# Both halves of a tile's scores issued one behind the other, the transposes of P behind them

## The chip, the cores and the metric

One core of a Trainium2 chip runs the whole program. The metric is the device time of one execution in microseconds (us); three executions of the kernel before gave a median of 1829.21 us.

## The reference

A network of two layers over `x` of shape (4, 512, 128). Each layer adds `s * silu(g)` to `x`, where `s` is a mixer and `g` a network, both computed from the layer-normed `x`. The change lies in the network of the first layer: six blocks of windowed attention (16 heads of 64, windows of 32 tokens, each query sees its own and the previous window) and a gated feed-forward part.

```python
def attn_layer(x, Wqkv, qs, ksc, Wo):
    q, k, v = heads(x @ Wqkv)                 # 16 heads of 64
    q, k = l2norm(q) * qs, l2norm(k) * ksc    # then rotary turn with a scale
    sim = einsum('bhwie,bhwje->bhwij', bq, look(bk)) * 8.0     # windows of 32, look: previous + own
    attn = softmax(where(mask, -max, sim), -1)
    out = einsum('bhwij,bhwje->bhwie', attn, look(bv))
    return out.reshape(b, n, INNER) @ Wo
for i in range(6):
    x = attn_layer(shift_tokens(x), ...) + x
    x = ffn_layer(shift_tokens(x), ...) + x
```

## The kernel before

`build_network` writes out, by hand, one instruction order for each engine. The unit of work is a tile of 128 tokens (four tiles to a batch, four batches, six blocks: 96 tiles). The engines all walk through the same numbered stages `g`; in stage `g` TensorE projects q, k and v of tile `g`, transposes q and k of tile `g-1` and forms its scores, transposes the softmax P of tile `g-2`, and multiplies P with v of tile `g-3` (`attend`). A round is the four tiles of one batch in one block. The work of a round that is no longer per tile is spread over the stages behind it, by the remainder of `g` by 4:

- remainder 2: the output projection in two halves, `output_projection(out_0, 0)` (called wo0 below) and `output_projection(out_1, 1)` (wo1), 16 matmuls each;
- remainder 3: `ffn_centre` and `ffn_variance`, the two matmuls of the layer norm; here `transpose_p(g-2, 0)` stands ahead of both score halves, and the halves already follow one another;
- remainder 0: `ffn_up` in three parts, in between the rest;
- remainder 1: `ffn_down`.

The names used below. **S0 and S1** are `scores(g-1, 0)` and `scores(g-1, 1)`, line 589: 64 small matmuls each, with a weight load to each, contraction over 64 rows, 32 columns of the array. They write `sc_ps`. Only S1's last matmul signals (`sc_full`), and S0 carries all the waits. **T0 and T1** are `transpose_p(g-2, 0)` and `transpose_p(g-2, 1)`, line 603: four 128x128 transposes each, each half waiting for its half of P (`p_scaled`, GpSimd line 496) and for a bank of `ring`.

`ring` is two PSUM banks taken in turn by everything in `stage_fills`; a fill waits until the fill two before it has been copied out. In stages of remainder 3 the fills end xc, p0, var, p1, so T1 waits for the copy of T0's output (`copy_pT(g-2, 0)`, ScalarE line 784). In stages of remainder 1 T1 waits for `add_ffn` (VectorE line 996).

VectorE's order in a stage: `add_attention(out_1, 1)` (line 973, only in remainder 3, it waits for wo1), then `row_max(g-2)` (lines 916, 918, 927; it waits for `sc_full`), `rotate` of k (951, 955), `sum_squares` of k (965), `row_sum(g-2)` (934, 939), `rotate` and `sum_squares` of q. ScalarE's end of a stage is `inverse_norms(g)` (lines 799, 801, 805; it waits for both sums of squares) and only behind it `copy_pT(g-2, 0)` (784), `inverse_deviation`, `copy_pT(g-2, 1)`. GpSimd scales P (496) after `row_sum`.

Of the kernel before, what the change touches and what calls it, by code (L numbers as in the profile page):

```python
# [267 lines left out]
def build_network(nc, block, signals, tail, weights, after, norm, state):  # L268
# [3 lines left out]
    with ctx:  # L272
# [81 lines left out]
        def tile_there(g):  # L354
            return 0 <= g < TILE_COUNT

        def round_at(g, s, later):

            r = g // TILES - later
            return r if g % TILES == s and 0 <= r < ROUNDS else None  # L360
# [161 lines left out]
        def _(pe):  # L522
# [14 lines left out]
            def project_q(g, f):  # L537

                if f == 1:
                    if g % (B * TILES) == 0:  # L540
                        pe.wait_ge(s_wq, 16 * (g // (B * TILES) + 1))
                    state_there(g)
                    if g > 0:
                        pe.wait_ge(q_sq, g)
                        pe.wait_ge(q_rot, 2 * g)
                nc.tensor.matmul(qk_ps[:, f, :], tile_of(g), quarter(wqkv, f), start=True, stop=True).then_inc(q_full, 1)  # L546

            def project_k(g, f):
                if f == 1:
                    if g % (B * TILES) == 0:  # L550
                        pe.wait_ge(s_wk, 16 * (g // (B * TILES) + 1))
                    state_there(g)
                    if g > 0:
                        pe.wait_ge(k_sq, g)
                        pe.wait_ge(k_rot, 2 * g)
                nc.tensor.matmul(qk_ps[:, 2 + f, :], tile_of(g), quarter(wqkv, 2 + f), start=True, stop=True).then_inc(k_full, 1)  # L556

            def project_v(g, f):
                if f == 0:
                    if g % (B * TILES) == 0:  # L560
                        pe.wait_ge(s_wv, 16 * (g // (B * TILES) + 1))
                    state_there(g)
                nc.tensor.matmul(ring_bank("v", g, f), tile_of(g), quarter(wqkv, 4 + f), start=True, stop=True).then_inc(v_full, 1)  # L563

            def transpose_qk(g, f):

                pe.wait_ge(qk_scaled, 4 * g + scale_at[f] + 1)
                to = ring_bank("t", g, f)
                for n in range(4):
                    c = 4 * f + n  # L570
                    ins = nc.tensor.transpose(to[:, n * P:(n + 1) * P], qkn[:, c * P:(c + 1) * P], ident[:, :])  # L571
                ins.then_inc(qkT_full, 1)

            def scores(g, f):

                t = g % TILES
                if f == 0:
                    if g == 0:
                        pe.wait_ge(c_dve, 8)
                        pe.wait_ge(tail.s_there.sem, 2 * TILES)  # L580
                    pe.wait_ge(qkT_copied, 4 * (g + 1))
                    if g == 1:
                        pe.wait_ge(sc_sub, 2)
                    if g > 1:
                        pe.wait_ge(oT_copied, 2 * (g - 1))
                for pair in range(4 * f, 4 * (f + 1)):
                    for q in range(TW):
                        for par in range(2):
                            ins = nc.tensor.matmul(  # L589
                                sc_ps[WIN * q:WIN * (q + 1), par, 64 * pair:64 * (pair + 1)],  # L590
                                qT[64 * par:64 * (par + 1), pair, WIN * q:WIN * (q + 1)],
                                kT[64 * par:64 * (par + 1), pair, P * t + WIN * q:P * t + WIN * (q + 2)],
                                start=True, stop=True)
                if f == 1:
                    ins.then_inc(sc_full, 1)
# [49 lines left out]
            def ffn_up(r, c):  # L645
                m = FCH[c]
                if c == 0:
                    pe.wait_ge(s_wffn, 48 * (r // B + 1))
                    pe.wait_ge(xn_ready, r + 1)
                nc.tensor.matmul(ring_bank("gate", r, c)[0:m, :], w1[:, FF + P * c:FF + P * c + m], xn[:, :],  # L650
                                 start=True, stop=True).then_inc(gate_full, 1)
                nc.tensor.matmul(ring_bank("lin", r, c)[0:m, :], w1[:, P * c:P * c + m], xn[:, :],
                                 start=True, stop=True).then_inc(lin_full, 1)
# [8 lines left out]
            for g in range(STAGES):  # L662
                out_0 = round_at(g, 2, 1)
                out_1 = round_at(g, 2, 1)
                centre = round_at(g, 3, 1)
                spread = round_at(g, 3, 1)
                up = round_at(g, 0, 2)
                down = round_at(g, 1, 2)
                if g == 0:
                    tail.turn_out(pe, 1)  # L670
                if tile_there(g):
                    project_k(g, 1)
                    project_k(g, 0)
                    if g == 1:
                        tail.turn_out(pe, 2)
                    project_v(g, 0)
                if g == 0:
                    pe.wait_ge(tail.r_og.sem, TILES)
                if g == 1:
                    tail.out_product(pe, 2)  # L680
                if tile_there(g - 1):
                    transpose_qk(g - 1, 3)
                if tile_there(g):
                    project_q(g, 1)
                if tile_there(g - 1):
                    transpose_qk(g - 1, 2)
                if g == 1:
                    tail.turn_out(pe, 3)
                if tile_there(g):
                    project_q(g, 0)  # L690
                if g == 1:
                    tail.out_product(pe, 3)
                if up is not None:
                    ffn_up(up, 0)
                if tile_there(g - 3):
                    attend(g - 3, 0)
                if tile_there(g - 1):
                    transpose_qk(g - 1, 1)
                if g == 0:
                    tail.out_product(pe, 1)  # L700
                if tile_there(g):
                    project_v(g, 1)
                if up is not None:
                    ffn_up(up, 1)
                if tile_there(g - 3):
                    attend(g - 3, 1)
                if tile_there(g - 1):
                    transpose_qk(g - 1, 0)
                if down is not None:
                    ffn_down(down)  # L710
                if centre is not None:
                    ffn_centre(centre)
                if g == TILE_COUNT + 3:

                    pe.wait_ge(q_sq, TILE_COUNT)
                    pe.wait_ge(k_sq, TILE_COUNT)
                    pe.wait_ge(q_rot, 2 * TILE_COUNT)
                    pe.wait_ge(k_rot, 2 * TILE_COUNT)
                    norm.centre(pe, 0, qk_ps[:, 0, :], centre_w)
                    norm.centre(pe, 1, qk_ps[:, 1, :], centre_w)  # L720
                if up is not None:
                    ffn_up(up, 2)
                if out_0 is not None:
                    output_projection(out_0, 0)
                if tile_there(g - 2) and centre is not None:
                    transpose_p(g - 2, 0)
                if tile_there(g - 1):
                    scores(g - 1, 0)
                if tile_there(g - 2) and centre is None:
                    transpose_p(g - 2, 0)  # L730
                if out_1 is not None:
                    output_projection(out_1, 1)
                if tile_there(g - 1):
                    scores(g - 1, 1)
                if spread is not None:
                    ffn_variance(spread)
                if g == TILE_COUNT + 3:
                    norm.centre(pe, 2, qk_ps[:, 2, :], centre_w)
                    norm.variance(pe, 0, qk_ps[:, 3, :], mean_w)
                if g == TILE_COUNT + 4:  # L740

                    pe.wait_ge(oT_copied, 2 * TILE_COUNT)
                    norm.variance(pe, 1, sc_ps[:, 0, :], mean_w)
                    norm.variance(pe, 2, sc_ps[:, 1, :], mean_w)
                if tile_there(g - 2):
                    transpose_p(g - 2, 1)
# [1675 lines left out]
```

## Time and profile before

| | |
|---|---|
| median of three executions | 1829.21 us (1826.84 to 1832.83) |
| span of the profiled execution | 1822.0 us |
| time outside the span, by the median | 7.2 us |
| TensorE matmul busy | 96% |
| VectorE busy | 80% |
| GpSimd busy | 65% |
| ScalarE busy | 64% |
| mean granted TensorE clock | 0.986 |

The span is counted from the first to the last instruction of one profiled execution; the executions that gave the median were timed as a whole, so the 7.2 us hold what lies around the span and the scatter of single executions. A busy TensorE is not TensorE at its peak: the share counts a matmul from its start to its modelled end.

### The profile page before, as it was taken

The page shows a single profiled execution, that of the slowest core. Times are in us where ns is not written, and L with a number is a line of the kernel's source. Part 1 is how long each engine was busy: PE and PEld are TensorE (multiplying, and loading weights), DVE is VectorE, ACT ScalarE, POOL GpSimd, SP SyncE. Part 2 cuts the span into 40 slices and gives each one's busy share as a digit, 9 for nine tenths or more (in the row PEclk, how much of TensorE's full clock was granted, in tenths as well). Part 3 has the DMA queues.
Part 4 walks back from the last instruction along what each step waited for, and adds up shares of the span by engine and source line. Part 5 has one row for each costly group of instructions (what it writes and reads, how often), then busy time and mean ns, then how long its engine had stood idle before and what let it go on. Part 6 is the DMA issues. An engine that isn't in the chain of part 4 may idle for free. (4 is left out here: it accounts for less than half of the span.)

```text
span 1822.0 us, 70687 instructions
## 1 busy us (share of the span) xinstructions
PE 1755.0 (96%) x30348; PEld 1136.7 (62%) x30348; DVE 1454.4 (80%) x1677; ACT 1162.8 (64%) x2032; POOL 1190.7 (65%) x1285
## 2 busy tenths in 40 slices
PE   7988999999999999999999999999999999998788
PEld 6855665665666566566666666656656656665466
DVE  6488789888788888888868978888887887896485
ACT  4356667667666765766766766676576676675644
POOL 1059678787677777767767867777776777775000
PEclk9899999999999999999999999999999999999999
DMA  4023222323222333223223223223223232222031
GB/s 151 1 50 77 58 72 66 92 66 80 73 68 68 95 78 73 73 57 98 73 67 80 68 64 98 67 69 80 72 60 91 70 81 69 65 68 74 1 71 47
DMA packets 87669, 128.94 MB, mean 71 GB/s; under 512 B 26776, under 2 KB 32800, under 8 KB 87360
## 3 DMA queue, kind: packets, MB, share of 16 engines
q1 hardware_dynamic: 87360, 124.43, 26.6%
q8 instruction: 242, 3.96, 1.0%
q14 instruction: 67, 0.55, 0.1%
HBM read 25.70 MB, written 1.11 MB: 15 GB/s over the span
## 5 line engine op out<-in xcount | busy, mean ns | idle before, releaser
L488 POOL TENSOR_TENSOR lent<-t,lent 128x1024 f32<-128x1024 f32 x192 | 455.2, 2371 | 356.7 <-DVE lent L955 356.6
L479 POOL TENSOR_TENSOR lent<-lent,rn 128x512 f32<-128x512 f32 x384 | 400.7, 1075 | 13.8
L619 PEld LDWEIGHTS sc_ps<-shared,v_win 64*64 64x64 f32 x12288 | 198.0, 135 | 147.1 <-issue 146.1
L791 ACT ACTIVATE sq<-qk_ps 128x1024 f32<-128x1024 f32 x192 | 196.1, 1021 | 94.9 <-PE qk_ps L556 94.2
L571 PEld LDWEIGHTS ring<-ident,lent 128*128 128x128 f32 x1536 | 176.5, 141 | 118.5 <-issue 76.8
L571 PE MATMUL ring<-ident,lent 128*128 128x128 f32 x1536 | 241.7, 280 | 5.7 <-POOL lent L479 5.3
L496 POOL TENSOR_TENSOR shared<-shared,rden 128x512 f32<-128x512 f32 x192 | 196.4, 1044 | 68.8 <-DVE rden L939 68.8
L784 ACT COPY shared<-ring 128x512 f32<-128x512 f32 x192 | 111.3, 580 | 198.2 <-PE ring L603 197.5
L955 DVE TENSOR_TENSOR lent<-qk_ps,rot 128x1024 f32<-128x1024 f32 x192 | 232.5, 1211 | 0.0
L965 DVE TENSOR_REDUCE sums<-sq 128x16 f32<-128x1024 f32 x192 | 231.7, 1207 | 0.0
L951 DVE TENSOR_TENSOR t<-qk_ps,rot 128x1024 f32<-128x1024 f32 x192 | 229.2, 1194 | 1.9 <-ACT sq L791 1.8
L619 PE MATMUL sc_ps<-shared,v_win 64*64 64x32 f32 x12288 | 219.1, 221 | 4.1 <-DVE shared L927 3.4
L546 PE MATMUL qk_ps<-wqkv,state 128*128 128x512 f32 x384 | 197.8, 597 | 0.2 <-DVE shared L1538 0.2
L563 PE MATMUL ring<-wqkv,state 128*128 128x512 f32 x384 | 196.9, 594 | 0.0
L589 PEld LDWEIGHTS sc_ps<-kT,qT 64*32 64x32 f32 x12288 | 136.9, 105 | 82.9 <-issue 77.0
L589 PE MATMUL sc_ps<-kT,qT 64*32 64x64 f32 x12288 | 166.2, 224 | 17.2 <-issue 11.8
L556 PE MATMUL qk_ps<-wqkv,state 128*128 128x512 f32 x384 | 182.2, 597 | 0.5 <-issue 0.5
L916 DVE TENSOR_TENSOR sc_ps<-sc_ps,mask_f 128x1024 f32<-128x1024 f32 x96 | 118.3, 1232 | 77.8 <-PE sc_ps L589 76.9
L634 PE MATMUL ring<-shared,wo 128*128 128x256 f32 x768 | 173.6, 379 | 0.0
L754 ACT COPY shared<-sc_ps 128x512 f32<-128x512 f32 x192 | 113.0, 589 | 71.3 <-PE sc_ps L619 71.3
L634 PEld LDWEIGHTS ring<-shared,wo 128*128 128x128 f32 x768 | 142.2, 190 | 17.4
L973 DVE TENSOR_TENSOR xa<-ring,state 64x256 f32<-64x256 f32 x96 | 40.6, 423 | 131.8 <-PE ring L634 130.3
(213 smaller groups left out, 2736.4 us busy)
## 6 DMA issues: line engine op xcount, KB each, us to landing
v_win<-v_tok SPq DMA_DIRECT2D x1488, 64.0 KB, 2.0
wqkv<-in_w_qkv SPq DMA_DIRECT2D x18, 512.0 KB, 3.7
spread<-gate_rows SPq DMA_DIRECT2D x32, 128.0 KB, 3.7
wo<-in_w_o SPq DMA_DIRECT2D x6, 512.0 KB, 3.8
w<-in_w SPq DMA_DIRECT2D x6, 341.0 KB, 3.3
w<-in_w SPq DMA_DIRECT2D x6, 192.0 KB, 3.0
r_xtok<-in_x SPq DMA_DIRECT2D x4, 256.0 KB, 3.9
out_x<-xo SPq DMA_DIRECT2D x4, 256.0 KB, 2.3
```

The lines of the kernel that those rows point to most:

```text
L479: nc.gpsimd.tensor_tensor(by_head(quarter(qkn, f)), by_head(quarter(qkn, f)), rn[:, 8 * f:8 * (f + 1)].unsqueeze(2).to_broadcast([P, 8, DH ...
L488: nc.gpsimd.tensor_tensor(half(qkn, k), half(t1, k), half(t2, k), ALU.add).then_inc((q_added, k_added)[k], 1)
L496: nc.gpsimd.tensor_tensor(by_head(quarter(pn, f)), by_head(quarter(pe_, f)), rden[:, 8 * f:8 * (f + 1)].unsqueeze(2).to_broadcast([P, 8, D ...
L546: nc.tensor.matmul(qk_ps[:, f, :], tile_of(g), quarter(wqkv, f), start=True, stop=True).then_inc(q_full, 1)
L563: nc.tensor.matmul(ring_bank("v", g, f), tile_of(g), quarter(wqkv, 4 + f), start=True, stop=True).then_inc(v_full, 1)
L571: ins = nc.tensor.transpose(to[:, n * P:(n + 1) * P], qkn[:, c * P:(c + 1) * P], ident[:, :])
L589: ins = nc.tensor.matmul(sc_ps[WIN * q:WIN * (q + 1), par, 64 * pair:64 * (pair + 1)], qT[64 * par:64 * (par + 1), pair, WIN * q:WIN * (q ...
L619: ins = nc.tensor.matmul(sc_ps[64 * par:64 * (par + 1), part, P * pair + WIN * q:P * pair + WIN * (q + 1)], v_win[64 * part:64 * (part + 1 ...
L634: ins = nc.tensor.matmul(to[:, 0:2 * P], wo[:, c, :], oT[:, c, 2 * P * f:2 * P * (f + 1)], start=(c == 0), stop=(c == PAIRS - 1))
L951: nc.vector.tensor_tensor(by_head(half(t1, k)), by_head(of), rot[:, l % 2, 2 * k, s:s + 1, :].to_broadcast([P, HEADS, DH]), ALU.mult).then ...
L955: nc.vector.tensor_tensor(half(t2, k).rearrange("p (h s d) -> p h s d", s=2, d=DH // 2), swapped, rot[:, l % 2, 2 * k + 1, s:s + 1, :].to_ ...
L965: nc.vector.tensor_reduce(sums[:, HEADS * k:HEADS * (k + 1)], by_head(half(sq, k)), AX.X, ALU.add).then_inc(sums_ready, 1)
```

## The change

In each stage S1 moves to directly behind S0. In the stages of remainder 0 and 1 the order S0 T0 S1 T1 becomes S0 S1 T0 T1. In the stages of remainder 2 wo0 S0 T0 wo1 S1 T1 becomes wo0 S0 S1 T0 wo1 T1. In the stages of remainder 3 (T0 S0 S1 var T1) nothing changes. The order of the ring's fills, all waits and the orders of the other engines stay.

```diff
                 if tile_there(g - 1):
                     scores(g - 1, 0)
+                if tile_there(g - 1):
+                    scores(g - 1, 1)
                 if tile_there(g - 2) and centre is None:
                     transpose_p(g - 2, 0)
                 if out_1 is not None:
                     output_projection(out_1, 1)
-                if tile_there(g - 1):
-                    scores(g - 1, 1)
                 if spread is not None:
                     ffn_variance(spread)
```

## Rows read from the trace of the kernel before

**Rows 1.** The page: the span, and each engine's busy time and instruction count.
```profile
span 1822.0 us, 70687 instructions
PE 1755.0 (96%) x30348; PEld 1136.7 (62%) x30348; DVE 1454.4 (80%) x1677; ACT 1162.8 (64%) x2032; POOL 1190.7 (65%) x1285
```

**Rows 2.** Timeline (start us, us, engine, line), end of a stage of remainder 1.
```profile
968.10 0.86 PE L589 MATMUL sc_ps<-kT,qT 64*32 64x64 f32 x64
968.20 1.53 DVE L996 SCALAR_TENSOR_TENSOR state<-ring,col,xa 64x512 f32<-64x512 f32 x2 [0.56 <-PE ring L659]
...
969.47 0.86 PE L589 MATMUL sc_ps<-kT,qT 64*32 64x64 f32 x64
...
970.75 1.88 PE L556 MATMUL qk_ps<-wqkv,state 128*128 128x512 f32 x4
```

**Rows 3.** Timeline, TensorE, end of a stage of remainder 2.
```profile
983.64 0.87 PE L589 MATMUL sc_ps<-kT,qT 64*32 64x64 f32 x64
984.43 0.66 PE L603 MATMUL ring<-ident,shared 128*128 128x128 f32 x4
984.93 3.62 PE L634 MATMUL ring<-shared,wo 128*128 128x256 f32 x16
988.48 0.86 PE L589 MATMUL sc_ps<-kT,qT 64*32 64x64 f32 x64
989.27 0.66 PE L603 MATMUL ring<-ident,shared 128*128 128x128 f32 x4
989.76 1.88 PE L556 MATMUL qk_ps<-wqkv,state 128*128 128x512 f32 x4
```

**Rows 4.** Timeline, TensorE, end of the stage behind it (remainder 3).
```profile
1000.03 0.63 PE L603 MATMUL ring<-ident,shared 128*128 128x128 f32 x4
...
1000.58 1.56 PE L589 MATMUL sc_ps<-kT,qT 64*32 64x64 f32 x128
...
1002.08 1.12 PE L643 MATMUL ring<-xsq,mean_w 128*128 128x512 f32 x2
...
1003.06 0.63 PE L603 MATMUL ring<-ident,shared 128*128 128x128 f32 x4
```

**Rows 5.** Timeline, VectorE, GpSimd and ScalarE from wo1 to that last transpose.
```profile
988.58 0.88 DVE L973 TENSOR_TENSOR xa<-ring,state 64x256 f32<-64x256 f32 x2 [3.96 <-PE ring L634]
...
989.52 1.23 DVE L916 TENSOR_TENSOR sc_ps<-sc_ps,mask_f 128x1024 f32<-128x1024 f32 x1
...
998.22 2.05 POOL L496 TENSOR_TENSOR shared<-shared,rden 128x512 f32<-128x512 f32 x2 [0.17 <-DVE rden L939]
...
1000.26 1.21 DVE L965 TENSOR_REDUCE sums<-sq 128x16 f32<-128x1024 f32 x1
...
1001.50 0.33 ACT L799 ACTIVATE raised<-sums,low_col 128x32 f32<-128x32 f32 x1
...
1002.35 0.57 ACT L784 COPY shared<-ring 128x512 f32<-128x512 f32 x1
```

**Rows 6.** The page: instruction fetch (DMA queues) and the scores' matmuls (costliest groups).
```profile
q8 instruction: 242, 3.96, 1.0%
L589 PE MATMUL sc_ps<-kT,qT 64*32 64x64 f32 x12288 | 166.2, 224 | 17.2 <-issue 11.8
```

**Rows 7.** Timeline, TensorE, holes inside a burst of scores: two of remainder 3, one of 0.
```profile
931.44 1.44 PE L589 MATMUL sc_ps<-kT,qT 64*32 64x64 f32 x114
935.25 0.34 PE L589 MATMUL sc_ps<-kT,qT 64*32 64x64 f32 x14 [2.37 <-issue]
...
1395.91 0.45 PE L589 MATMUL sc_ps<-kT,qT 64*32 64x64 f32 x29 [1.37 <-issue]
...
1547.97 0.38 PE L589 MATMUL sc_ps<-kT,qT 64*32 64x64 f32 x18 [1.51 <-issue]
```

**Rows 8.** Timeline and stretches (busy us by engine, PEclk, DMA): clock behind the first hole.
```profile
937.20 3.29 PE L556 MATMUL qk_ps<-wqkv,state 128*128 128x512 f32 x4
936.50:940.00 3.50, 3.50 (x9) 1.95 (x8) 3.43 (x5) 1.79 (x3) 2.72 (x3) 0.52 0.38 97
```

## The prediction

> **What bounds the kernel now.** First the page: TensorE is busy for 96% of the span, the next engine, VectorE, for 80% [rows 1]. So nearly all of the time is TensorE's own queue, and a step taken out of it counts in full where no other engine's result arrives just as late. Then the timeline of each kind of stage, to price a step from start to start, since the modelled ends overlap. Then, for each wait that TensorE passes near the change, how long the awaited work had been done. Last the holes in which TensorE waits for no engine ("issue").
>
> Two things stand beside TensorE's own work. **A chain that is exactly as late.** In a stage of remainder 3, T1 starts 0.14 us after the end of copy_pT(0) (1002.35 + 0.57 = 1002.92, T1 at 1003.06) [rows 4, 5]. That copy stands on ScalarE behind inverse_norms, which starts at 1001.50, 0.03 us after VectorE's last sum of squares (1000.26 + 1.21 = 1001.47). VectorE has run without a gap since it took up wo1's sums at 988.58. So wo1 is the head of a chain: wo1, VectorE's whole stage, inverse_norms, the copy, T1. From wo1's start (984.93) to T1 (1003.06) it takes 18.13 us [rows 3, 4]. I read the same distance in all 23 such rounds: from copy to T1 it is 0.14 to 0.30 us in 17 of them, 0.41 in one, and 1.6 to 4.0 in the five in which a hole kept TensorE back first. 0.14 is the smallest, and where it stands TensorE comes up to 0.03 us later behind var than its own pace would have it, so 0.14 is the latency and TensorE and the chain tie.
>
> **Holes of instruction supply.** Scores run at 11 ns a matmul, each with a load. Inside such bursts TensorE stops for up to 2.6 us with nothing to wait for [rows 6, 7]. The fetch queue moved 3.96 MB in 242 packets, 16.4 KB each, for 60,696 loads and matmuls [rows 1, 6], one packet for 251 of them, and with the waits in between one for 256. Numbering the queue's records by start, all 12 holes within bursts fall on the same point of the 256. So they are late blocks. Where they stop, the block's packet had landed 1.2 to 1.5 us before; it starts typically 0.8 us after the block before it began to be used and takes 0.9 to 1.5 us. A block thus needs some 3 to 4 us, and 256 instructions used up faster than that make a hole.
>
> **The change part by part.** (1) Fewer changes between scores and transposes on TensorE. Before, the tail of a stage is S0 and T0 1.37, S1 and T1 1.28 = 2.65 us (968.10 to 970.75) [rows 2]. Both score halves together, up to the next operation, take 1.50 (1000.58 to 1002.08) [rows 4], where two apart take 2 x 0.79 [rows 3]. A transpose half ahead of ordinary work takes 0.49, ahead of scores 0.55 to 0.59 [rows 2 to 4]. After: 1.50 + 0.49 + 0.49 = 2.48, a gain of 0.17. In the stages of remainder 2, wo1 takes 3.55 ahead of scores; at its step of 0.216 (3.62 less a last 0.38, over 15) it takes 3.46 ahead of T1: 0.79 + 0.50 + 3.55 + 0.79 + 0.49 = 6.12 becomes 1.50 + 0.50 + 3.46 + 0.49 = 5.95, again 0.17 [rows 3]. 72 stages change (24 of remainder 0, 23 of 1, 24 of 2, and the one of 3 that has no centre): **-12.2 us**. T0 directly before T1 isn't in the trace. At 0.44, its shortest case, it would be -16; at 0.59, as ahead of scores, -5.
>
> (2) wo1 is moved. With S1 ahead of it, it starts and ends 1.50 - 0.79 = 0.71 later in 23 rounds. VectorE starts add_attention on it, as before (3.96 us idle ahead of it [rows 5]), so T1 of the next stage can't start before +0.71, while TensorE, 0.17 early, arrives at -0.17. Per round TensorE waits 0.88 less the slack above. 18 rounds have 0.00 to 0.27 of it, 0.7 us together: 18 x 0.88 - 0.7 = **+15.1 us**; in the five with a hole the wait lies within the hole. Bounds: 0 if VectorE could start its stage early, 23 x 0.88 = 20 if no hole covers. I take 15, since all 23 chains measure alike. Behind T1 nothing of it is given back: k's projections, T1's successors, stand in the same queue.
>
> (3) More and longer holes. The stretch S0 T0 S1 took 0.79 + 0.59 + 0.79 = 2.16 us; now 128 scores take 1.50, and in the remainder-2 stages wo1 no longer parts them. I laid the 242 blocks over the new order and kept each block's supply time as traced: holes grow from 17 to 24 us. With supply times drawn at random from those traced, the growth is 5 to 12. I take **+6.5 us**, with 0 and +20 as bounds: the high end comes from the stages of remainder 3, where scores already run as 128: five of 23 have a hole of 1.4 to 2.6 us within the burst [rows 7], far more than the others.
>
> (4) Clock. Behind the 2.37 us hole TensorE runs at a granted 0.52, its lower level, and k's four matmuls take 3.29 in place of 1.88 us [rows 2, 8]; behind the holes of up to 2.0 us it does not fall. One more fall, some 1.5 us, is possible; taken at nothing.
>
> (5) At nothing: T0 0.7 later (its copy isn't late for attend, a stage away, nor for v's bank, over 1.5 us behind T1); T1 0.17 earlier (in remainder 1 it waits for add_ffn, done at 969.73, its own start 970.26 [rows 2, 3]: 0.53 of cover, and without it at most 0.17 x 23 = 4); T0 of remainder 3, whose half of P is done at 999.24, 0.79 ahead of it [rows 4, 5]: 0.88 later that is 0.1 to 0.15 late, but it lies within the wait at T1. row_max starts up to 0.7 earlier in the stages of remainder 1 and 2, which only gives VectorE slack. No DMA is issued by what moves, and SP, GpSimd, VectorE and ScalarE keep their order. The one wait that grows is T1's of remainder 3. Behind it stand T1 and the next stage's projections; for those wait squares and rotate.
>
> **Sum**, against the span of 1822.0: -12.2 + 15.1 + 6.5 = +9.4, so 1831.4. With 7.2 around it by the median, 1829.2 + 9.4 = **1838.6 us**.
>
> [...] Holes of over 1.3 us stand in the middle of bursts [rows 7]. [...]
>
> **Rivals.** (A) TensorE alone decides: the chain gives way, because VectorE makes up the 0.71, and holes grow little. -12.2 + 3 = -9, 1820. For it: 96% busy, VectorE only 80%. Against it: VectorE is gapless for 12 us in just this stage. 0.07. [...] (B) The chain binds, but holes don't grow, or T0 to T1 runs at 0.44: 1829.2 - 12.2 + 15.1 = 1832, down to 1829 with the shorter step, within 0.3%. 0.17. (C) Slower by holes above all: the changed stages come near the rate of those of remainder 3, +20 for term (3) and some falls of the clock. It decides once a block of 256 takes longer than 1.5 us plus what is queued before it, as those rows show it can: 1829.2 + 2.9 + 20 + 3 = 1855. 0.06. (D) The forecast, slower by 6 to 18 us: 0.70. That the change doesn't do what it says is hardly possible here, since TensorE keeps the order of its matmuls.
>
> **How the numbers follow.** 0.3% is 5.5 us, about what a measurement of this kernel can tell from no change. Faster: A, 0.07. Same: B, 0.17, and little of D. Slower: D and C, 0.76. The forecast's own range, from its terms' bounds, is 1833 to 1847. Leaving out A's lower half and C, the range is 1829 to 1848.
>
> **What would show it.** In the profile after: from S to the next operation 1.50 in changed stages, T0 to T1 0.49; wo1 starting 1.50 + 0.50 behind S0; 18.13 from wo1 to T1 unchanged; TensorE waiting about 0.7 to 0.9 us ahead of T1 in remainder 3, on the copy of line 784; rounds longer by about a third of a microsecond where no hole falls; holes of line 589 adding up to 20 to 30 us, some now in stages of remainder 2. It would be wrong if VectorE's stage behind wo1 became shorter than 12 us, if T0 and T1 waited for each other, or if holes came where none is computed.

## The result

The changed kernel takes 1837.38 us (median of 22 executions) against 1830.71 us for the kernel before (22 executions): 0.42% slower, with a 95% interval of 0.27% to 0.57%, that is 5 to 10 us. Forecast were 9.4 us more and 1838.6 us. The change loses by one mechanism and gains by another, as laid out in the prediction; the sizes are compared below. Two single executions of the kernels tried below (3534 and 3411 us, near twice the others) are left out of every ratio.

The page of the changed kernel, first lines and three of its costliest groups:

```profile
span 1835.8 us, 70687 instructions
PE 1754.4 (96%) x30348; PEld 1144.5 (62%) x30348; DVE 1454.9 (79%) x1677; ACT 1161.6 (63%) x2032; POOL 1190.6 (65%) x1285
...
L589 PE MATMUL sc_ps<-kT,qT 64*32 64x64 f32 x12288 | 162.4, 225 | 25.6 <-issue 20.4
...
L973 DVE TENSOR_TENSOR xa<-ring,state 64x256 f32<-64x256 f32 x96 | 40.6, 423 | 158.2 <-PE ring L634 156.7
...
L916 DVE TENSOR_TENSOR sc_ps<-sc_ps,mask_f 128x1024 f32<-128x1024 f32 x96 | 118.3, 1232 | 42.7 <-PE sc_ps L589 41.4
```

The same two groups of VectorE on the page of the kernel before:

```profile
L916 DVE TENSOR_TENSOR sc_ps<-sc_ps,mask_f 128x1024 f32<-128x1024 f32 x96 | 118.3, 1232 | 77.8 <-PE sc_ps L589 76.9
L973 DVE TENSOR_TENSOR xa<-ring,state 64x256 f32<-64x256 f32 x96 | 40.6, 423 | 131.8 <-PE ring L634 130.3
```

Not one instruction more, and no engine has more work than in [rows 1]. What moved is waiting: VectorE waits 158 us ahead of the projection's sums in place of 132, the stop of the scores at "issue" (TensorE waits for no engine) has grown from 11.8 to 20.4 us [rows 6], and the mask, first step of row_max, waits 43 us in place of 78. The two profiled executions are 13.8 us apart, twice as far as the medians. The execution profiled before was the fastest of its 22 (1824.09 us: what lies around its span of 1822.0 is 2 us; the 7.2 us outside the span in the table of the time before were mostly scatter), and the holes, stops of TensorE in which it waits for no engine, differ from execution to execution. So lengths of stages are compared below, not spans.

A stage's length, from the start of k's projections (line 556) to the next, median over stages 8 to 91, in us:

| remainder | before | after | only 0 and 1 changed | only 2 changed | 2 changed, row_max first |
|---|---|---|---|---|---|
| 0 | 17.48 | 17.33 | 17.31 | 17.48 | 17.57 |
| 1 | 14.67 | 14.48 | 14.53 | 14.67 | 14.67 |
| 2 | 19.00 | 18.94 | 19.00 | 18.99 | 18.97 |
| 3 | 13.74 | **14.68** | 13.75 | **14.68** | 13.74 |

The only stage that got longer is the one in which nothing was edited. First the tail (the end, from S0 on) of a stage of remainder 1, on TensorE's timeline (start, us, engine, line); it answers to [rows 2]:

```profile
974.93 1.48 PE L589 MATMUL sc_ps<-kT,qT 64*32 64x64 f32 x128
976.34 1.09 PE L603 MATMUL ring<-ident,shared 128*128 128x128 f32 x8
977.27 1.88 PE L556 MATMUL qk_ps<-wqkv,state 128*128 128x512 f32 x4
```

128 scores, then T0 and T1 as one row of eight, 0.93 us together. From S0 to k's projections it is 2.34 us here and 2.47 in the median stage of remainder 1, against 2.65 before. Then the stage of remainder 2 and the tail of the one behind it; it answers to [rows 3, 4]:

```profile
990.16 1.68 PE L589 MATMUL sc_ps<-kT,qT 64*32 64x64 f32 x128
991.77 0.66 PE L603 MATMUL ring<-ident,shared 128*128 128x128 f32 x4
992.26 3.62 PE L634 MATMUL ring<-shared,wo 128*128 128x256 f32 x16
995.72 0.60 PE L603 MATMUL ring<-ident,shared 128*128 128x128 f32 x4
996.16 1.88 PE L556 MATMUL qk_ps<-wqkv,state 128*128 128x512 f32 x4
...
1006.62 0.66 PE L603 MATMUL ring<-ident,shared 128*128 128x128 f32 x4
1007.21 1.55 PE L589 MATMUL sc_ps<-kT,qT 64*32 64x64 f32 x128
1008.68 1.13 PE L643 MATMUL ring<-xsq,mean_w 128*128 128x512 f32 x2
1010.36 0.63 PE L603 MATMUL ring<-ident,shared 128*128 128x128 f32 x4 [0.55 <-ACT shared L784]
```

The last row is where the loss comes due: T1 waits 0.55 us for ScalarE's copy, which it never did before. The other 0.4 of the 0.94 us lie ahead of it: T0 starts 0.2 us later behind the centre matmul, and the 128 scores take 1.55 us from first to last start in place of 1.35. Without these two T1 would have waited that much longer, since the chain sets its start. From wo1's start (992.26) to this T1 it is 18.10 us, as before (18.13). The chain itself, on VectorE and ScalarE, against [rows 5]:

```profile
995.92 0.88 DVE L973 TENSOR_TENSOR xa<-ring,state 64x256 f32<-64x256 f32 x2 [4.78 <-PE ring L634]
996.83 1.23 DVE L916 TENSOR_TENSOR sc_ps<-sc_ps,mask_f 128x1024 f32<-128x1024 f32 x1
...
1007.57 1.21 DVE L965 TENSOR_REDUCE sums<-sq 128x16 f32<-128x1024 f32 x1
...
1008.81 0.32 ACT L799 ACTIVATE raised<-sums,low_col 128x32 f32<-128x32 f32 x1 [0.89 <-issue]
...
1009.65 0.57 ACT L784 COPY shared<-ring 128x512 f32<-128x512 f32 x1
```

VectorE waits 4.78 us for wo1 where it waited 3.96, then runs without a gap to 1008.78; inverse_norms starts 0.03 us later, the copy ends at 1010.22, T1 starts 0.14 us behind it. In 16 of 23 rounds T1 waits for the copy; it stands 0.14 us behind it in 15 of them and 0.26 in one. In the other seven a hole had kept TensorE back, and T1 starts 0.45 to 2.73 us behind the copy.

The holes and the clock. Two of the holes on TensorE's timeline, in stages of remainder 3 and 0, with what comes behind the first:

```profile
673.37 1.38 PE L589 MATMUL sc_ps<-kT,qT 64*32 64x64 f32 x105
676.96 0.42 PE L589 MATMUL sc_ps<-kT,qT 64*32 64x64 f32 x23 [2.21 <-issue]
...
679.36 2.92 PE L556 MATMUL qk_ps<-wqkv,state 128*128 128x512 f32 x4
...
826.36 1.64 PE L589 MATMUL sc_ps<-kT,qT 64*32 64x64 f32 x122
829.88 0.31 PE L589 MATMUL sc_ps<-kT,qT 64*32 64x64 f32 x6 [1.88 <-issue]
```

And a stretch behind the first of them (window, its length, busy us of each engine, granted clock, DMA share, GB/s):

```profile
678.20:681.20 3.00, 3.00 (x8) 1.66 (x7) 2.93 (x5) 1.79 (x3) 3.00 (x4) 0.50 0.38 97
```

The second hole stands in a stage of remainder 0, where the burst was parted before. To add the holes up, take at the same point of every block of 256 instructions by how much the step there exceeds the usual one, where the block's packet had landed less than 1.7 us before. That gives 16.9 us in the execution before, 26.3 in this one and 28.2 in a second one of the changed kernel. What is taken as the usual step moves such a sum by up to 2 us: with the median over the same pair of lines the three are 18.7, 26.5 and 29.1. The clock stands at its lower level (a granted 0.50) behind three of the holes (from 678.0, 1210.5 and 1408.5 us on, 3.4 us each) where it did behind two, in one execution of each kernel.

### The profile page after: what moved, and what is told of

It is laid out like the page before. It is cut to its first block and busy times, and to the rows that moved or that the text cites. A ratio compares the mean times of both kernels' runs of the same rounds, so it can differ in the third digit from the quotient of the medians.

```text
span 1835.8 us, 70687 instructions
## 1 busy us (share of the span) xinstructions
PE 1754.4 (96%) x30348; PEld 1144.5 (62%) x30348; DVE 1454.9 (79%) x1677; ACT 1161.6 (63%) x2032; POOL 1190.6 (65%) x1285
## 3 DMA queue, kind: packets, MB, share of 16 engines
q1 hardware_dynamic: 87360, 124.43, 26.3%
q8 instruction: 242, 3.96, 0.9%
## 5 line engine op out<-in xcount | busy, mean ns | idle before, releaser
L479 POOL TENSOR_TENSOR lent<-lent,rn 128x512 f32<-128x512 f32 x384 | 401.1, 1076 | 13.8
L784 ACT COPY shared<-ring 128x512 f32<-128x512 f32 x192 | 107.0, 583 | 209.9 <-PE ring L603 208.8
L589 PE MATMUL sc_ps<-kT,qT 64*32 64x64 f32 x12288 | 162.4, 225 | 25.6 <-issue 20.4
```

Of the source, the lines that this page charges most:

```text
L479: nc.gpsimd.tensor_tensor(by_head(quarter(qkn, f)), by_head(quarter(qkn, f)), rn[:, 8 * f:8 * (f + 1)].unsqueeze(2).to_broadcast([P, 8, DH ...
L589: ins = nc.tensor.matmul(sc_ps[WIN * q:WIN * (q + 1), par, 64 * pair:64 * (pair + 1)], qT[64 * par:64 * (par + 1), pair, WIN * q:WIN * (q ...
```

## The experiments

Each run is timed beside the kernel before on the same chip; ratios are against that, with a 95% interval. The last column is the ratio less 1 times the median of the kernel before; it can differ by some us from the difference of the medians (6.7 us for the full change). 0.1% is 1.8 us.

| kernel | ratio to before | interval | us |
|---|---|---|---|
| full change | 1.0042 | 1.0027 to 1.0057 | +7.7 |
| full change, second comparison | 1.0032 | 1.0014 to 1.0051 | +5.9 |
| remainder 0 and 1 alone | 0.9992 | 0.9973 to 1.0010 | -1.5 |
| remainder 2 alone | 1.0098 | 1.0065 to 1.0131 | +17.9 |
| remainder 2 alone, row_max first | 1.0002 | 0.9982 to 1.0023 | +0.4 |
| remainder 2 alone, scores behind wo1 | 1.0061 | 1.0042 to 1.0080 | +11.2 |
| full change, copy first | 1.0037; 1.0015 | 1.0017 to 1.0057; 1.0000 to 1.0029 | +6.8; +2.7 |
| full change, row_max first | 0.9986; 0.9968 | 0.9968 to 1.0005; 0.9952 to 0.9984 | -2.6; -5.9 |
| remainder 2 with row_max first, halves parted in 3 | 1.0039 | 1.0020 to 1.0057 | +7.1 |

### Which stages lose

The theory was that wo1, pushed back behind S1, heads a chain that T1 of the next stage must wait for. The rival was that bursts of 128 scores cost wherever they stand, by holes. So the change was made in one kind of stage at a time.

```diff
                 if tile_there(g - 1):
                     scores(g - 1, 0)
+                if tile_there(g - 1) and out_1 is None:
+                    scores(g - 1, 1)
                 if tile_there(g - 2) and centre is None:
                     transpose_p(g - 2, 0)
                 if out_1 is not None:
                     output_projection(out_1, 1)
-                if tile_there(g - 1):
+                if tile_there(g - 1) and out_1 is not None:
                     scores(g - 1, 1)
```

> Only the stages without an output projection are changed (S0 S1 T0 T1 in remainder 0 and 1); in remainder 2 the order stays wo0 S0 T0 wo1 S1 T1. Chain theory (the loss comes from wo1 being pushed back behind S1): wo1 isn't moved, TensorE does not wait ahead of T1 in remainder 3, and only the gain of some 0.11 us a stage less the longer holes is left: -5 to +2 us against the kernel before. Rival, holes alone (the loss comes from bursts of 128 scores wherever they are): these are two thirds of the changed stages, so two thirds of the loss, +4 to +5 us.

The second has `is None` and `is not None` exchanged.

> Only the stages of remainder 2 are changed (wo0 S0 S1 T0 wo1 T1). Chain theory: the whole loss stands here, some 0.8 us in each of the about 18 rounds without a hole in remainder 3, so +9 to +14 us against the kernel before, more than the full change; the stages of remainder 3 take 14.67 us instead of 13.74. Rival, holes alone: a third of the loss, +2 to +3 us.

Measured: -1.5 us (-4.9 to +1.8) and +17.9 us (11.9 to 23.9). The loss comes with the 23 changed stages of remainder 2 alone, and it is bigger there than in the full change and than was expected (+9 to +14). In its profile, TensorE, the stage of remainder 3:

```profile
1011.24 1.13 PE L643 MATMUL ring<-xsq,mean_w 128*128 128x512 f32 x2
1012.88 0.63 PE L603 MATMUL ring<-ident,shared 128*128 128x128 f32 x4 [0.52 <-ACT shared L786]
```

The same wait on the same copy, and 14.68 us for the stage. The rival would have given +4 to +5 and +2 to +3. It is refuted as the cause of the loss: in the second run's profile the holes are no longer than before (17.7 against 18.7 us, both by the median over the same pair of lines). It is not refuted as a term: with remainder 0 and 1 alone the tails are shorter by the 0.18 us a stage that the full change shows, some 8 us in 49 stages, and 1.5 are left, while holes stand at 25.5 us against 16.9. In the second, 16 rounds wait as in the full change, and 0.94 x 16 is 15 us. The profiled execution is 15.0 us above the median of the kernel before on that chip (1841.62 against 1826.66), and 15 lies within the interval of the timing, which rests on five executions. Whether anything beyond the 15 us is lost isn't shown.

### Taking the chain's head off wo1

With the change, the scores of remainder 2 are complete before wo1 starts, while VectorE waits 4.78 us for wo1. On VectorE alone, row_max was moved ahead of the projection's sums:

```diff
+                if tile_there(g - 2):
+                    row_max(g - 2)
                 if out_1 is not None:
                     add_attention(out_1, 1)
                 if g == TILE_COUNT + 3:
                     norm.gated_x1(dve, 2)
-                if tile_there(g - 2):
-                    row_max(g - 2)
```

> The full change, and on VectorE row_max(g-2) is put ahead of add_attention(out_1, 1). With the change the scores of remainder 2 are done some 4 us before wo1, while VectorE sits idle for 3.96 us waiting for wo1, so that row_max (3.7 us) fits into that gap. Chain theory: VectorE's stage of remainder 3 is no longer bound to wo1's end plus row_max, T1 doesn't wait, and the stage falls back to 13.7 us or less: 12 to 16 us faster than the full change, so -5 to -9 us against the kernel before. Rival, holes alone: like the full change, +7 us. Rival, the gain goes to the next wait (the first transpose of k in the next stage): -3 to +2 us.

> Remainder 2 alone changed (wo0 S0 S1 T0 wo1 T1), with row_max ahead of add_attention(out_1, 1) on VectorE. Chain theory: row_max moves into VectorE's idle time ahead of wo1's end, the wait ahead of T1 goes, 14 to 18 us faster than the same kernel without it, so -4 to +3 us against the kernel before. Rival: the loss of that kernel has another cause (holes, pace of the burst) and stays, +12 us or more.

The timeline of the first, VectorE, then ScalarE's copy and T1, then two rows of the next stage:

```profile
991.03 1.23 DVE L916 TENSOR_TENSOR sc_ps<-sc_ps,mask_f 128x1024 f32<-128x1024 f32 x1 [0.84 <-PE sc_ps L589]
...
993.56 1.29 DVE L927 TENSOR_TENSOR shared<-sc_ps,smax 128x512 f32<-128x512 f32 x2
...
995.08 0.88 DVE L973 TENSOR_TENSOR xa<-ring,state 64x256 f32<-64x256 f32 x2 [0.23 <-PE ring L634]
...
998.29 1.23 DVE L951 TENSOR_TENSOR t<-qk_ps,rot 128x1024 f32<-128x1024 f32 x1 [2.33 <-ACT sq L791]
...
1007.81 0.57 ACT L784 COPY shared<-ring 128x512 f32<-128x512 f32 x1
...
1008.59 0.60 PE L603 MATMUL ring<-ident,shared 128*128 128x128 f32 x4
...
1013.16 1.15 DVE L983 TENSOR_SCALAR xn<-xc,col 128x512 f32<-128x512 f32 x1
...
1014.40 1.10 PE L650 MATMUL ring<-xn,w 128*128 128x512 f32 x2
```

row_max now fills the time in which wo1 runs (991.42 to 994.9). VectorE then waits 2.33 us for the squares of k, so the chain begins at k's projections and no longer at wo1: from wo1's start to T1 it is 17.17 us in place of 18.10, and T1 stands 0.2 us behind the copy where 0.14 is the latency: free, but barely. The stage of remainder 3 is back at 13.8 us. With remainder 2 alone this one reordering takes the loss of 17.9 us away (+0.4 left, within the -4 to +3 expected).

On the full change it gave -2.6 us. That misses the -5 to -9 expected and lies within what the second rival said (-3 to +2), that the gain goes to the next wait. The last two rows show such a wait, though not at the transpose of k that the rival named: `ffn_up` (line 650) starts 0.09 us behind the end of xn (1013.16 + 1.15 = 1014.31), where before it had 0.45 us to spare. In the median stage of remainder 0 it starts 5.30 us behind k's projections in place of 5.17, and the stage takes 17.40 us in place of 17.33 (17.54 in the second execution below). VectorE's step ahead of xn (line 978) takes 1.47 us there in place of 0.95 before and 0.68 with the full change; why was not tried. The second comparison, beside the full change on the same chip:

> The full change once more, unaltered, as the neighbour of the next two on the same chip: +5 to +10 us against the kernel before.

> The full change with row_max ahead of add_attention(out_1, 1), once more: 8 to 12 us faster than the full change beside it and 1 to 5 us faster than the kernel before. If it comes out level with the full change, the first comparison was scatter.

Measured +5.9 and -5.9 us: 11.8 us between the two (9.5 by the medians), as expected, and a little more than the 1 to 5 us expected against the kernel before. It is faster than that kernel with its whole interval here (-8.8 to -2.9); in the first comparison the interval still reached +0.9.

### Cutting the last link instead

The chain holds T1 only because the copy of T0's output is queued on ScalarE behind inverse_norms. In stages of remainder 3, it was put ahead:

```diff
+                if tile_there(g - 2) and centre is not None:
+                    copy_pT(g - 2, 0)
                 if tile_there(g):
                     inverse_norms(g)
-                if tile_there(g - 2):
+                if tile_there(g - 2) and centre is None:
                     copy_pT(g - 2, 0)
```

> The full change, and on ScalarE, in the stages of remainder 3 alone, the copy of T0's output (line 784) is put ahead of inverse_norms. It takes out the one link by which the chain from wo1 holds T1. Chain theory: T1 no longer waits; what is left of the delay is the first transpose of k in the next stage, which had 0.5 us of cover against a chain that is 0.88 late, so some 0.35 us a round are still lost there: 7 to 11 us faster than the full change, -3 to +1 us against the kernel before. Rival, TensorE's own pace or holes set the loss: no difference from the full change, +7 us.

> The full change with ScalarE's copy of T0's output ahead of inverse_norms in remainder 3, once more. Its first profile shows T1 free (1.5 us behind the copy) and the stage of remainder 3 at 14.16 us in place of 14.67, but the next stage at 17.56 in place of 17.33, because its first transpose of k now waits for GpSimd: 0.28 us a round less, 6 us. Chain theory with a second link: 3 to 7 us faster than the full change beside it. Rival (the chain costs nothing, other than in the profile): no difference.

The first comparison gave +6.8 us against before, no better than the full change: a miss by its expectation. The second gave +2.7, 3.1 us under the full change beside it (2.1 by the medians), at the low end of what the second expectation said, with intervals that overlap. The timeline of the second, over ScalarE, TensorE and GpSimd:

```profile
1006.87 0.57 ACT L784 COPY shared<-ring 128x512 f32<-128x512 f32 x1
...
1008.71 0.60 PE L603 MATMUL ring<-ident,shared 128*128 128x128 f32 x4
...
1010.83 3.67 POOL L479 TENSOR_TENSOR lent<-lent,rn 128x512 f32<-128x512 f32 x3
...
1010.86 1.02 PE L563 MATMUL ring<-wqkv,state 128*128 128x512 f32 x2
...
1011.93 0.65 PE L571 MATMUL ring<-ident,lent 128*128 128x128 f32 x4
```

The copy is done 1.3 us ahead of T1, the wait is gone and the stage takes 14.16 to 14.18 us, but the late chain goes on over inverse_norms and GpSimd to the next stage: v's projection would let the transpose of k start at 1011.72 (0.86 behind 1010.86, as from 1012.55 to 1013.41 in the full change), and it starts at 1011.93, 0.06 us behind the end of the first of GpSimd's three multiplications in that row, which takes 1.04. That stage grows from 17.33 to 17.56 us. Together 0.28 us a round are won, 6 us in 23 rounds, not the 7 to 11 first expected. The stage of remainder 3 stays 0.4 us longer than before by what the wait at T1 had hidden: T0's own wait for GpSimd, 0.2, and the slower burst, 1.55 in place of 1.35. The stages show the size; the timing shows no more than its sign, at best.

### Putting the scores behind wo1

The same burst in remainder 2, without pushing wo1 back (wo0 T0 wo1 S0 S1 T1):

```diff
-                if tile_there(g - 1):
+                if tile_there(g - 1) and out_1 is None:
                     scores(g - 1, 0)
                 if tile_there(g - 2) and centre is None:
                     transpose_p(g - 2, 0)
                 if out_1 is not None:
                     output_projection(out_1, 1)
+                if tile_there(g - 1) and out_1 is not None:
+                    scores(g - 1, 0)
```

> As the kernel before, but in the stages of remainder 2 both score halves stand together BEHIND wo1 (wo0 T0 wo1 S0 S1 T1). The burst on TensorE is the same as in the run that changed remainder 2 alone; only wo1 isn't pushed back, it even comes some 0.8 us earlier. Chain theory (place of wo1): stage of remainder 3 stays at 13.7 us, and the time is that of the kernel before or up to 4 us less, so some 18 us under the run with the scores ahead of wo1. Rival (a burst of 128 scores in remainder 2 is what costs, by holes and pace): as slow as that run, +10 to +18 us.

Measured +11.2 us, where up to -4 was expected and the rival said +10 to +18. The number alone would speak for the rival. The timeline of TensorE and VectorE in remainder 2 says otherwise:

```profile
994.41 0.60 PE L603 MATMUL ring<-ident,shared 128*128 128x128 f32 x4
994.61 0.88 DVE L975 TENSOR_TENSOR xa<-ring,state 64x256 f32<-64x256 f32 x2 [1.43 <-PE ring L634]
995.63 3.69 PE L634 MATMUL ring<-shared,wo 128*128 128x256 f32 x16 [0.62 <-DVE xa L975]
```

wo1 takes the bank of wo0 and waits until VectorE has added wo0 up (0.88 us). S0 and T0 between the two, 1.28 us, had covered that; T0's 0.49 alone doesn't. The stage of remainder 2 takes 19.69 us in place of 19.00, 0.69 x 23 = 16 us, while the stage of remainder 3 stands at 13.80 as expected and holes at 18.7 us. So the timing doesn't test what it was made for, since the order swapped one wait for another that the plan had overlooked. The stages do: a burst of 128 scores in remainder 2 leaves the stage of remainder 3 as it was when wo1 isn't pushed back behind it.

### The holes

First a longer queue with the same work: extra matmuls ahead of the very first scores, into cells that the scores overwrite.

```diff
+                if f == 0 and g == 0:
+                    for n in range(32):
+                        nc.tensor.matmul(sc_ps[0:WIN, 0, 0:64], qT[0:64, 0, 0:WIN], kT[0:64, 0, 0:64], start=True, stop=True)
```

That is the edit of the second run below. The first had `range(64)`:

> The full change, with 64 further small matmuls and their loads ahead of the first scores, which write what is overwritten right behind them: 128 more instructions in TensorE's queue, and nothing else moved. Supply theory: holes stay at number 194 of each 256 instructions of this queue, which is 64 score matmuls away from where they are in the full change: the burst of the stage with 107 matmuls ahead of its hole gets it after 43, those that have it after some 50 get none or one after some 114; sum 18 to 32 us. Rival (holes hang on an operand, a bank or the place in the stage): the same stages and the same places in the burst as before.

Every call left two matmuls and two loads, so this one moved the blocks by exactly 256 instructions. Of the 14 places with a hole within a burst of scores in the full change (stage and matmul), 11 came back to within five matmuls, so the expectation's places were wrong and the run, one execution, can't tell the two theories apart. With `range(32)`, half a block and again one execution:

> The full change with half of the extra matmuls of the run before: in that run each call left two matmuls and two loads, so the queue was longer by 256 instructions, one whole block, and the holes stood in the same stages and at the same matmul of the burst as without it, which says nothing. Here it is longer by 128, half a block. Supply theory: all holes in bursts still stand at number 193 or 194 of each 256 of this queue, but in other places: the stages with a hole behind matmul 115 to 126 of their 128 (stages 7, 21, 44, 65, 67, 81, 88) lose it or keep a short one some 64 matmuls earlier, and other stages get one in the second half of their burst; sum 15 to 32 us. Rival (the hole hangs on what is computed there): the same stages and the same matmuls.

All 14 places are gone, and eight others have one, each at number 193 or 194 of a block of this queue, in eight stages none of which had one before. On its timeline, TensorE, two of the new ones:

```profile
350.73 0.24 PE L592 MATMUL sc_ps<-kT,qT 64*32 64x64 f32 x1 [1.80 <-issue]
...
694.26 1.61 PE L592 MATMUL sc_ps<-kT,qT 64*32 64x64 f32 x117
697.79 0.33 PE L592 MATMUL sc_ps<-kT,qT 64*32 64x64 f32 x11 [1.92 <-issue]
```

With those just behind the bursts the holes add up to 20.6 us. They hang on the instruction's number, not on what is computed: in all 14 profiles, every stop of over 0.15 us within a half of scores stands at number 193 or 194 of its 256.

Then less of a burst: the halves parted by T0 in remainder 3 (S0 T0 S1 var T1) and, as before, in 0 and 1, on top of remainder 2 with row_max first.

```diff
-                if tile_there(g - 2) and centre is not None:
-                    transpose_p(g - 2, 0)
                 if tile_there(g - 1):
                     scores(g - 1, 0)
...
-                if tile_there(g - 2) and centre is None:
+                if tile_there(g - 2):
                     transpose_p(g - 2, 0)
```

> Scores together only in remainder 2, ahead of wo1, with row_max first on VectorE; in remainder 3 the halves are parted by T0 (S0 T0 S1 var T1), in remainder 0 and 1 as in the kernel before. Supply theory (a burst of 128 pairs uses up a block of 256 instructions before the next has come): the holes of remainder 3 shrink by the 0.6 us that T0 puts between, from some 11 us in all to 4 to 7, at a price of 0.1 us a stage for the two further changes of kind; -1 to -7 us against the kernel before. Rival (a hole's length does not depend on what stands within the block): holes as before, +1 to +4 us.

Holes were 18.3 us in place of 21.8 (remainder 2 with row_max first), one execution each, where two executions of the full change differ by 1.9. That is a hint at most that they shrank, and the kernel takes +7.1 us, outside both the -1 to -7 expected and the rival's +1 to +4. ScalarE and TensorE in remainder 3:

```profile
1006.17 0.59 ACT L754 COPY shared<-sc_ps 128x512 f32<-128x512 f32 x1
...
1006.90 0.85 PE L589 MATMUL sc_ps<-kT,qT 64*32 64x64 f32 x64 [0.39 <-ACT shared L754]
```

S0 writes `sc_ps` and waits until the result of `attend` has been copied out of it. T0, which needs no such bank, had filled that wait. The stage takes 14.31 us in place of 13.74, 13 us in 23 rounds against 3.5 of holes.

## Why the prediction was right, step by step

- **Fewer changes between scores and transposes, -12.2 us.** Its two halves were off in opposite ways. T0 to T1 takes 0.49 us as written, but T1 to k's projections 0.44 in place of 0.49 (eight transposes in 0.93). The burst of 128 takes 1.61 us in the median changed stage, not 1.50: its first half runs at the old pace, 64 in 0.64 us, its second is slower, and why isn't shown. The sum holds in remainder 0 and 1 (-0.18 a stage), in remainder 2 it is -0.06 where -0.17 was written. In all some 10 us. What a change of kind costs can be read from the steps: a half of transposes takes 0.44 us where a transpose or wo1 stands ahead of it and 0.49 where scores do, and 0.59 where scores stand on both sides. Why it costs that isn't shown.
- **wo1 pushed back, +15.1 us.** Right in mechanism, place and size: the chain from wo1 to T1 kept its length (18.13 and 18.10), and the stage of remainder 3 grew by 0.94 where 0.88 was computed. The 0.06 is the step from T1 of remainder 2 to k's projections, 0.44 in place of 0.49: the stage is counted from k's projections, which come that much sooner behind wo1, while the chain doesn't. The two parts of the 0.88 were off in opposite ways: wo1 is pushed back by 0.88 us behind S0, not 0.71, because the burst ahead of it takes 1.67 us, and for the same reason TensorE comes 0.06 us early and not 0.17. That the place of wo1 is the cause is shown by three runs: no wait without the change in remainder 2, the wait with it alone, and none with row_max first.
- **Longer holes, +6.5 us.** +9.4 and +11.3 in two executions against the one profiled before (+7.8 and +10.4 with the other usual step), within the bounds given. The laying out of blocks was right in kind (a hole in stage 44, of remainder 0, that had none, those of stages 65, 81 and 88 0.6 to 0.9 us longer), and too low in size. One row was misread in it: of the five holes put within bursts of remainder 3, four are; the fifth stands at the transposes behind one (478.28 us). The step across a hole reached 2.8 us in these bursts (at 213.26 us in the execution before). The block of 256 stands by the packets, 242 of 16,384 bytes for the 61,912 records of this queue, waits included, and by the half-block run.
- **Clock, nothing.** One more fall in the profiled execution, as said to be possible, 1.0 to 1.4 us by the 2.92 and 3.29 us in place of 1.88 [rows 2, 8]. A second execution of the changed kernel has one such fall, where before has two, so that the change adds falls isn't shown. A hole's length alone doesn't decide it: behind 2.09 and 2.40 us it stayed up, behind 2.18, 2.21 and 2.43 it fell.
- **At nothing.** T1 in remainder 1 isn't held by add_ffn. T0 of remainder 3 starts 1.12 us behind the centre matmul in place of 0.93, 0.2 late where 0.1 to 0.15 was written, within T1's wait.
- **The sum.** The stages of remainder 3 less their holes are 14 to 17 us longer in the two executions of the changed kernel, falls of the clock included, so -10 + 14 to 17 + 8 to 11 would be 12 to 18. That is near the 13.8 and 12.4 us between their spans and that of before, and above the 5 to 10 us of the timing. The kernel before varies over 13 us, from 1824.09 to 1837.34, and its profiled execution was the fastest of all 22. A mean over executions would probably have given the hole term less, which one trace of that kernel can't show. That the forecast of 9.4 us came out near is in part luck: it added growth over the fastest execution to the median, and took the hole term low.
- **The range.** 1833 to 1847 doesn't follow from the bounds of the terms: these give 1813 (-16, 0, 0) to 1864 (-5, +20, +20) around 1829.2 us. The measured time lies within the narrower range too.

## What to carry to other kernels

Where a bottleneck engine's queue is reordered, what is pushed back can matter more than what is packed together (here +17.9 us with remainder 2 alone, -1.5 with 0 and 1 alone): look for the step in the moved stretch that another engine waits for, follow it to where it comes back to this queue, and compare with the slack there, also when that is a stage in which nothing was edited. A reordering can open an idle time elsewhere (here 4.8 us of VectorE ahead of wo1), and the gain was only had here when the other engine's order was changed with it. Before a step is taken out from between two others, list what its time was hiding, such as the copy that frees a bank or the wait of the next writer; two of these plans failed on that.

## What the runs showed of the hardware that was not expected

- In the 14 profiles TensorE stops within the bursts of scores at number 193 or 194 of a block of 256 instructions, with steps of 0.2 to 2.8 us. In 196 of the 197 stops of over 0.15 us it resumes 1.15 to 1.60 us after the last packet has landed; in the other one, a step of 0.17 us, 3.4 us after it. Shifting the queue by half a block moved all of the 14 holes, by a whole block three, in one execution each.
- A burst of 128 scores takes 1.35 us from first start to last in remainder 3 when T0 ahead of it starts without a wait for GpSimd (before, remainder 0 and 1 alone, row_max first), and 1.55 when T0 had to wait for it (full change, remainder 2 alone, copy first), in medians of 22 stages each. In the changed stages of remainder 0, 1 and 2 it takes 1.48, 1.39 and 1.52. The slower steps are in the second half of the burst. The cause was not tried.
